# Two bf16 products on constants in each tile of the second FFN's expert loop

## The chip, the core and the metric

The program runs on one core of one Trainium2 chip. The metric is the device time of one execution in microseconds (us); lower is better. The core's engines run side by side and wait for each other on semaphores: TensorE (PE; its weight loads are listed as PEld), VectorE (DVE), ScalarE (ACT), GpSimd (POOL), and SyncE (SP), whose queue issues most of the transfers.

## What is computed

A graph network with four pairs of a graph layer and a mixture-of-experts FFN on 3125 nodes of 256 features. The change is in the second FFN. Each node goes to one of 32 experts with a hidden width of 64, a quarter of the feature width:

```python
def _L1_ffn_ref(x, router_w, router_b, W1, b1, W2, b2):
    logits = xf @ router_w.T + router_b
    idx = jnp.argmax(logits, axis=-1)
    w1t = jnp.take(W1, idx, axis=0)          # W1: (32, 256, 64)
    h = jax.nn.relu(jnp.einsum('nd,ndh->nh', xf, w1t) + jnp.take(b1, idx, axis=0))
    w2t = jnp.take(W2, idx, axis=0)          # W2: (32, 64, 256)
    out = jax.nn.relu(jnp.einsum('nh,nhd->nd', h, w2t) + jnp.take(b2, idx, axis=0))
```

## The kernel before

The stages run one after the other: a graph layer (`layer`), then `route`, `run_experts` and `combine` of an FFN, and so on. `route` picks an expert for each node and POOL scatters the normed rows to slots sorted by expert, in tiles of 128 slots that belong to one expert each. `run_experts` then works through the tiles. `combine` gathers the results back to the nodes.

`run_experts` serves the first FFN (`m0`: 8 experts, hidden 256), the second (`m1`: 32 experts, hidden 64, 56 tiles) and the fourth (`m3`: 16 experts, hidden 512). FP is the smaller of 128 and the hidden width, so it is 64 in `m1` alone. The tiles are a software pipeline over the engines. PE's step for tile c is written out by hand (lines 1428 to 1447):

- `turn(c + 1)`, line 1413: two transposes of the next tile's rows, as products with the identity, into `tp`. VectorE copies them to `xt` (line 1492).
- the up products of tile c, line 1437: weights `wa`, moving `xt`, into `hp`. In `m1` they fill 128 rows and 64 columns of the array. ScalarE makes `h` of `hp` (line 1471).
- `down(c - 1)`, line 1423: weights `h` of the tile before, moving `wb`, into `yp`. In `m1` they fill 64 rows and 128 columns. VectorE adds the bias and takes the maximum with zero into `yo` (lines 1500 and 1505), and ACT's queue stores `yo` to `results`.

So what PE needs in a step from VectorE (the copy of tile c) and from ScalarE (`h` of tile c - 1) was asked for a step earlier. An f32 product appears in the trace as two instructions: line 1437 gives 4 in a step of `m1`, line 1413 gives 2, line 1423 gives 2. SP loads each tile's `wa` and `wb` eight tiles ahead (lines 1389 and 1392, each waits for the down of an earlier tile) and the rows of four tiles in one transfer (line 1382). VectorE waits before its second tile for the table of second biases, `b2b` (line 1399 loads it). `over` runs the steps, the first eight unrolled and the rest in a loop of eight.

Of the kernel before, what the change touches and what calls it, by code (L numbers as in the profile page):

```python
# [16 lines left out]
BF16 = mybir.dt.bfloat16  # L17
# [7 lines left out]
P = 128  # L25
# [1304 lines left out]
def run_experts(nc, k, m, func, w1, b1, w2, b2, relu_out, slots, results, meanwhile):  # L1330


    sem, F, FP, FB, E, n = k.sem, m.F, m.FP, m.FB, m.E, m.tiles
# [18 lines left out]
    with ExitStack() as scope:  # L1352
# [3 lines left out]
        def bank(n, shape):  # L1356
            return scope.enter_context(nc.psum_tensor(f"{m.name}_x_{n}", shape, F32))
# [8 lines left out]
        b1_given, b1t = sb("b1_given", [rows_b1, FP]), sb("b1t", [FP, rows_b1])  # L1366
        turn_psum, h_psum, y_psum = bank("tp", [P, 2, 512]), bank("hp", [FP, 2, 512]), bank("yp", [P, 2, 512])
        b1_psum = bank("b1p", [FP, rows_b1])
        with nc.Block() as block:
            meanwhile(block)  # L1370

            @block.sync
            def _(sp):
                sp.dma_start(b1_given[:], b1.rearrange("e (b f) -> (e b) f", f=FP)).then_inc(s["b1_in"], 16)
                experts = []

                def step(c, u, i, first):
                    if u % DEEP == 0:
                        count = min(DEEP, n - c) if isinstance(c, int) else DEEP
                        if not first:  # L1380
                            sp.wait_ge(s["turned"], c - DEEP)
                        sp.dma_start(xin[:, u:u + count, :],
                                     slots[bass.ds(c * P, count * P), :].rearrange("(t p) f -> p t f", p=P))\
                            .then_inc(rows_in[u // DEEP], 16)
                        experts[:] = experts_from(mybir.EngineType.SP, c)
                    e, v = experts[u % DEEP], u % W
                    if not first or u >= W:
                        sp.wait_ge(s["down"], c - W + 1)
                    sp.dma_start(wa[:, v, :, :], w1[bass.ds(e, 1), :, :].rearrange("e (b p) f -> p (e b) f", p=P))\
                        .then_inc(loaded[v], 16)  # L1390
                    if not all_w2:
                        sp.dma_start(wb[:, v, :, :],
                                     w2[bass.ds(e, 1), :, :].rearrange("e (b p) f -> p (e b) f", p=FP))\
                            .then_inc(loaded[v], 16)
                    if first and u == 0:
                        if all_w2:
                            sp.dma_start(wb[:, :, :, :].rearrange("p e b f -> p (e b) f"),
                                         w2.rearrange("e (b p) f -> p (e b) f", p=FP)).then_inc(w2_in, 16)
                        sp.dma_start(b2b[:], b2.partition_broadcast(P)).then_inc(b2_in, 16)
                over(sp, n, ROUND, step)  # L1400

            @block.tensor
            def _(pe):
                pe.wait_ge(s["b1_in"], 16)
                nc.tensor.transpose(b1_psum[:], b1_given[:], k.ident[0:rows_b1, 0:rows_b1]).then_inc(s["b1_turned"], 1)

                def turn(c, u, i, early):
                    if u % DEEP == 0:
                        pe.wait_ge(rows_in[u // DEEP], (i + 1) * 16)
                    if not early:  # L1410
                        pe.wait_ge(s["turned_sb"], c - 1)
                    for b in range(KD):
                        mm = nc.tensor.transpose(turn_psum[:, u % 2, b * P:(b + 1) * P],
                                                 xin[:, u, b * P:(b + 1) * P], k.ident[:])
                    mm.then_inc(s["turned"], 1)

                def down(c, u, early, e):
                    pe.wait_ge(s["hidden"], c + 1)
                    if not early:
                        pe.wait_ge(s["out"], c - 1)  # L1420
                    for f in range(FB):
                        w = wb[:, bass.ds(e, 1), f, :].rearrange("p e f -> p (e f)") if all_w2 else wb[:, u % W, f, :]
                        mm = nc.tensor.matmul(y_psum[:, u % 2, 0:D], h[:, u % 2, f, :], w,  # L1423
                                              start=(f == 0), stop=(f == FB - 1))
                    mm.then_inc(s["down"], 1)


                def step(c, u, i, first):
                    if not (isinstance(c, int) and c == n - 1):
                        turn(c + 1, (u + 1) % ROUND, i + (u + 1) // ROUND, first and u == 0)  # L1430
                    pe.wait_ge(s["turned_sb"], c + 1)
                    pe.wait_ge(loaded[u % W], (i * (ROUND // W) + u // W + 1) * per_tile)
                    if not first or u >= 2:
                        pe.wait_ge(s["hidden"], c - 1)
                    for f in range(FB):
                        for b in range(KD):
                            mm = nc.tensor.matmul(h_psum[:, u % 2, f * P:(f + 1) * P],  # L1437
                                                  wa[:, u % W, b, f * FP:(f + 1) * FP],
                                                  xt[:, u % 2, b * P:(b + 1) * P], start=(b == 0), stop=(b == KD - 1))
                    mm.then_inc(s["up"], 1)  # L1440
                    if all_w2 and u % DEEP == 0:
                        start = first and u == 0
                        experts[:] = [None] * start + list(experts_from(mybir.EngineType.PE, c if start else c - 1))
                    if all_w2 and first and u == 1:
                        pe.wait_ge(w2_in, 16)
                    if not first or u >= 1:
                        down(c - 1, (u - 1) % ROUND, first and u <= 2, experts[u % DEEP] if all_w2 else None)
                experts = []
                turn(0, 0, 0, True)
                over(pe, n, ROUND, step, last_apart=True)  # L1450
                down(n - 1, (n - 1) % ROUND, False, experts_from(mybir.EngineType.PE, n - 1)[0] if all_w2 else None)

# [29 lines left out]

            @block.vector
            def _(dve):
                dve.wait_ge(s["b1_turned"], 1)
                nc.vector.tensor_copy(b1t[:], b1_psum[:]).then_inc(s["b1"], 1)

                def copy(c, u, early):
                    dve.wait_ge(s["turned"], c + 1)
                    if not early:  # L1490
                        dve.wait_ge(s["up"], c - 1)
                    nc.vector.tensor_copy(xt[:, u % 2, :], turn_psum[:, u % 2, 0:D]).then_inc(s["turned_sb"], 1)

                def finish(c, u, i, e):
                    dve.wait_ge(s["down"], c + 1)
                    if not isinstance(c, int) or c >= DEEP:

                        dve.wait_ge(stored[u % DEEP // 2], (2 * i + u // DEEP) * 16)
                    to = yo[:, u % DEEP, :]
                    ins = nc.vector.tensor_tensor(to, y_psum[:, u % 2, 0:D],  # L1500
                                                  b2b[:, bass.ds(e, 1), :].rearrange("p e f -> p (e f)"), ALU.add)
                    if relu_out:
                        ins.then_inc(s["sum"], 1)
                        dve.wait_ge(s["sum"], c + 1)
                        ins = nc.vector.tensor_scalar(to, to, 0.0, None, ALU.max)
                    ins.then_inc(s["out"], 1)

                def step(c, u, i, first):
                    if not (isinstance(c, int) and c == n - 1):
                        copy(c + 1, u + 1, first and u == 0)  # L1510
                    if u % DEEP == 0:

                        start = first and u == 0
                        experts[:] = [None] * start + list(experts_from(mybir.EngineType.DVE, c if start else c - 1))
                    if not first or u >= 1:
                        finish(c - 1, (u - 1) % ROUND, i if u else i - 1, experts[u % DEEP])
                experts = []
                copy(0, 0, True)
                dve.wait_ge(b2_in, 16)
                over(dve, n, ROUND, step, last_apart=True)  # L1520
                finish(n - 1, (n - 1) % ROUND, (n - 1) // ROUND, experts_from(mybir.EngineType.DVE, n - 1)[0])
# [491 lines left out]
```

## Time and profile before

| | us |
|---|---|
| median of 3 runs | 4030.24 |
| range of the runs | 4023.66 to 4031.4 |
| the profiled execution | 3997.73 |
| its span, first to last instruction | 3995.8 |
| mean granted TensorE clock of it | 0.809 |

The profile is of one execution. Its own time is 1.9 us above its span, and 0.8% below the median of the runs. The granted clock is a share of the full 2.4 GHz: 1.00 is full, 0.50 is 1.2 GHz. Matmuls are pipelined, and each row's duration reaches to the modelled end of its last product, so that groups overlap in the rows; the distance from the start of one group to the start of the next is what counts.

### The profile page before, as it was taken

How to read it: one execution, taken by the hardware profiler on the slowest of the kernel's cores; microseconds unless marked ns; L12 is line 12 of the kernel's file. 1: busy time of each engine (PE TensorE's matmuls, PEld its weight loads, DVE VectorE, ACT ScalarE, POOL GpSimd, SP SyncE). 2: the span in 40 equal slices, each digit the busy share in tenths (PEclk: the TensorE clock that was granted, in tenths of full speed). 3: DMA queues.
4: the chain of work that ended last, by engine and by line, in shares of the span. 5: the costliest groups of instructions: out<-in, count | busy, mean ns of one | idle time of the engine just before them, and what ended most of it. 6: DMA issues, size and time to landing. Idle time of an engine off the chain costs nothing. (4 is left out here: it accounts for less than half of the span.)

```text
span 3995.8 us, 42625 instructions
## 1 busy us (share of the span) xinstructions
PE 2921.7 (73%) x12729; PEld 1717.6 (43%) x12730; DVE 1247.8 (31%) x4178; ACT 766.0 (19%) x1927; POOL 1561.7 (39%) x1107
## 2 busy tenths in 40 slices
PE   2344219889997482999899839599879499927980
PEld 1122104334446282444444515244469255526870
DVE  8899600004445334000300323300121500131126
ACT  4899500000002020100100101100133300012221
POOL 0788888836400574820650061583000300040005
PEclk6555559999996696999999755699889799958995
DMA  6899749679871394986897155599300344218983
GB/s 278 289 293 291 211 81 319 189 231 306 263 240 52 115 254 121 340 261 208 279 264 263 34 136 140 184 325 272 98 24 0 108 129 129 56 56 281 328 283 94
DMA packets 449643, 781.39 MB, mean 196 GB/s; under 512 B 157952, under 2 KB 298498, under 8 KB 439509
## 3 DMA queue, kind: packets, MB, share of 16 engines
q1 hardware_dynamic: 300372, 722.78, 52.1%
q0 software_dynamic: 124896, 33.44, 9.0%
q10 hardware_dynamic: 24224, 23.34, 1.7%
q8 instruction: 75, 1.23, 0.1%
q14 instruction: 76, 0.61, 0.0%
HBM read 604.33 MB, written 175.05 MB: 195 GB/s over the span
## 5 line engine op out<-in xcount | busy, mean ns | idle before, releaser
L789 PE MATMUL sum_psum<-abuf,y 128*128 128x512 f32 (+1 forms) x3500 | 1415.3, 564 | 320.1 <-ACT y L718 176.9
L789 PEld LDWEIGHTS sum_psum<-abuf,y 128*128 128x128 f32 x3500 | 627.1, 191 | 1088.8 <-issue 941.8
L561 POOL DMA_INDIRECT table_t<-sums,index_from x392 | 614.6, 1568 | 402.2 <-POOLq L1936 190.8
L561 POOL DMA_INDIRECT table_pairs<-sums,index_to x392 | 610.4, 1557 | 226.5 <-issue 116.3
L725 ACT ACTIVATE gathered<-sum_psum 128x512 f32<-128x512 f32 (+1 forms) x84 | 41.0, 540 | 1862.9 <-PE sum_psum L789 1862.9
L1137 POOL COPY y<-m_ybuf 128x256 f32 (+1 forms) x39 | 15.7, 402 | 759.8 <-ACT m_ybuf L1202 759.8
L1534 POOL DMA_INDIRECT m_c_rows<-results,slot_i x125 | 119.1, 953 | 474.6 <-PEq L1528 437.4
L789 PE MATMUL sum_psum<-abuf,acc 128*128 128x512 f32 (+1 forms) x700 | 290.0, 577 | 9.4 <-DMA abuf<-table_pairs 9.4
L1437 PE MATMUL m_x_hp<-m_x_xt,m_x_wa 128*128 128x128 f32 (+1 forms) x1720 | 255.4, 300 | 25.8 <-DMA m_x_wb<-in_L_ffn_W_dram 9.6
L1423 PE MATMUL m_x_yp<-m_x_wb,m_x_h 128*128 128x256 f32 (+2 forms) x860 | 252.9, 427 | 6.6 <-issue 6.6
L441 PE MATMUL merge_psum<-part,acc 128*128 128x6 bf16 x980 | 70.9, 167 | 241.8 <-DVE pass_on L515 124.0
L1471 ACT ACTIVATE m_x_h<-m_x_hp,m_x_b1t 128x128 f32<-128x128 f32 (+1 forms) x430 | 130.4, 367 | 582.8 <-PE m_x_hp L1437 574.7
L1437 PEld LDWEIGHTS m_x_hp<-m_x_xt,m_x_wa 128*128 128x128 f32 (+1 forms) x1720 | 221.8, 199 | 46.8 <-issue 26.6
L789 PEld LDWEIGHTS sum_psum<-abuf,acc 128*128 128x128 f32 x700 | 130.1, 201 | 165.2 <-issue 155.4
L441 PEld LDWEIGHTS merge_psum<-part,acc 128*128 128x128 bf16 x980 | 56.8, 104 | 325.0 <-issue 322.7
L485 DVE SCALAR_TENSOR_TENSOR acc<-row_psum,edge_key,acc 128x128 bf16<-128x128 f32 (+3 forms) x392 | 192.3, 546 | 1.4 <-PE row_psum L421 1.1
L465 ACT ACTIVATE away<-row_psum,edge_key 128x512 f32<-128x512 f32 x291 | 179.9, 699 | 63.6 <-PE row_psum L427 62.4
L469 ACT ACTIVATE acc<-away 128x512 bf16<-128x512 f32 x291 | 181.3, 648 | 0.0
L1423 PEld LDWEIGHTS m_x_yp<-m_x_wb,m_x_h 128*128 128x128 f32 (+1 forms) x860 | 162.5, 208 | 41.3 <-issue 27.5
L1323 POOL DMA_INDIRECT slots<-y,slot_i x125 | 125.0, 1000 | 100.6 <-DVE slot_i L1178 63.4
L835 DVE TENSOR_TENSOR acc<-out_psum,rows 128x256 f32<-128x256 f32 (+1 forms) x25 | 10.6, 423 | 427.7 <-PE out_psum L748 427.7
L1500 DVE TENSOR_TENSOR m_x_yo<-m_x_yp,acc 128x256 f32<-128x256 f32 x122 | 51.8, 425 | 279.3 <-PE m_x_yp L1423 256.6
(333 smaller groups left out, 2965.8 us busy)
## 6 DMA issues: line engine op xcount, KB each, us to landing
abuf<-table_pairs SPq DMA_DIRECT2D x750, 512.0 KB, 4.9
table_pairs<-zero SPq DMA_DIRECT2D x50, 1600.0 KB
table_t<-zero SPq DMA_DIRECT2D x25, 1600.0 KB
abuf<-table_t SPq DMA_DIRECT2D x150, 256.0 KB, 2.6
m_x_wa<-in_L_ffn_w_dram SPq DMA_DIRECT2D x65, 512.0 KB, 4.3
m_x_wb<-in_L_ffn_w_dram SPq DMA_DIRECT2D x65, 512.0 KB, 5.6
m_x_xin<-slots SPq DMA_DIRECT2D x44, 512.0 KB, 3.9
results<-m_x_yo ACTq DMA_DIRECT2D x88, 256.0 KB, 4.5
```

What stands on the lines that cost most here:

```text
L441: mm = nc.tensor.matmul(to, k.same[:, u % 2, at(j) + i * P:at(j) + (i + 1) * P], k.part[:, g, c.start + j, :], start=(j == i), stop=(u == ...
L465: nc.scalar.activation(k.away[:, j, :], next_rows(u + 1), ACT.Abs, bias=column(k.edge_key, u, j), scale=-1.0).then_inc(apart, 1)
L469: nc.scalar.activation(k.later[:, u % 3, j, :], k.away[:, j, :], ACT.Relu, bias=1.0, scale=-1.0, accum_out=column(k.more, u, j)).then_inc( ...
L485: nc.vector.scalar_tensor_tensor(k.same[:, u % 2, at(j):at(j + 1)], own_rows(u)[:, 0:(j + 1) * P], column(k.edge_key, u, j), k.mask[:, (BL ...
L561: nc.gpsimd.indirect_dma_start(table[:, :], bass.IndirectOffsetOnAxis(ap=index[:, g, j:j + 1], axis=0), k.sums[:, g, j, 0:width], None, co ...
L789: mm = nc.tensor.matmul(k.sum_psum[:, b % 2, f, 0:n], h[:, c, f * P:(f + 1) * P], operand(i % RING, c - q * QUART, n), start=(c == 0), sto ...
L1323: nc.gpsimd.indirect_dma_start(slots, bass.IndirectOffsetOnAxis(ap=k.slot_i[:, j:j + 1], axis=0), k.y[:, j // K, :], None).then_inc(s["lai ...
L1423: mm = nc.tensor.matmul(y_psum[:, u % 2, 0:D], h[:, u % 2, f, :], w, start=(f == 0), stop=(f == FB - 1))
L1437: mm = nc.tensor.matmul(h_psum[:, u % 2, f * P:(f + 1) * P], wa[:, u % W, b, f * FP:(f + 1) * FP], xt[:, u % 2, b * P:(b + 1) * P], start= ...
L1471: ins = nc.scalar.activation(h[:, u % 2, f, :], h_psum[:, u % 2, f * P:(f + 1) * P], func, bias=b1t[:, bass.ds(e * FB + f, 1)])
L1500: ins = nc.vector.tensor_tensor(to, y_psum[:, u % 2, 0:D], b2b[:, bass.ds(e, 1), :].rearrange("p e f -> p (e f)"), ALU.add)
L1534: nc.gpsimd.indirect_dma_start(rows[:, j % GROUP, :], None, results[0:m.tiles * P, :], bass.IndirectOffsetOnAxis(ap=k.slot_i[:, j:j + 1], ...
```

## The change

With FP below 128, which is `m1` alone, VectorE fills a tile `busy` of 128 x 512 bf16 with 0.5 at the start of the stage and counts a semaphore up, for which PE waits before its first instruction. In each step PE multiplies a 128 x 128 part of `busy` with all 512 columns of it, once after `turn(c + 1)` and once after the up products. Both write to a PSUM bank of their own that nothing reads. Nothing that is kept is computed otherwise than before.

```diff
+        narrow = FP < P
+        if narrow:
+            busy, busy_psum, busy_ready = sb("busy", [P, 512], BF16), bank("busyp", [P, 512]), sem(f"{m.name}_x_busy")
...
             @block.tensor
             def _(pe):
+                if narrow:
+                    pe.wait_ge(busy_ready, 1)
                 pe.wait_ge(s["b1_in"], 16)
...
                     if not (isinstance(c, int) and c == n - 1):
                         turn(c + 1, (u + 1) % ROUND, i + (u + 1) // ROUND, first and u == 0)
+                    if narrow:
+                        nc.tensor.matmul(busy_psum[:], busy[:, 0:P], busy[:], start=True, stop=True)
                     pe.wait_ge(s["turned_sb"], c + 1)
...
+                    if narrow:
+                        nc.tensor.matmul(busy_psum[:], busy[:, 0:P], busy[:], start=True, stop=True)
                     if not first or u >= 1:
                         down(c - 1, (u - 1) % ROUND, first and u <= 2, experts[u % DEEP] if all_w2 else None)
...
             @block.vector
             def _(dve):
+                if narrow:
+                    nc.vector.memset(busy[:], 0.5).then_inc(busy_ready, 1)
                 dve.wait_ge(s["b1_turned"], 1)
```

On PE, at the start of `m1`'s stage, the order of before is this (`tp` are the transposes, `hp` the up products, `yp` the down products; a row is one product with its output's shape):

```order
L1405 MATMUL m_x_b1p<-ident,m_x_b_given 64x32
L1413 MATMUL m_x_tp<-ident,m_x_xin 128x128 x4
L1437 MATMUL m_x_hp<-m_x_xt,m_x_wa 64x128 x2
L1413 MATMUL m_x_tp<-ident,m_x_xin 128x128 x2
L1437 MATMUL m_x_hp<-m_x_xt,m_x_wa 64x128 x2
L1423 MATMUL m_x_yp<-m_x_wb,m_x_h 128x256
```

And in the changed kernel, on PE at the same place:

```order
L1410 MATMUL m_x_b1p<-ident,m_x_b_given 64x32
L1418 MATMUL m_x_tp<-ident,m_x_xin 128x128 x4
L1437 MATMUL m_x_busyp<-m_x_busy 128x512
L1444 MATMUL m_x_hp<-m_x_xt,m_x_wa 64x128 x2
L1454 MATMUL m_x_busyp<-m_x_busy 128x512
L1418 MATMUL m_x_tp<-ident,m_x_xin 128x128 x2
L1437 MATMUL m_x_busyp<-m_x_busy 128x512
L1444 MATMUL m_x_hp<-m_x_xt,m_x_wa 64x128 x2
L1454 MATMUL m_x_busyp<-m_x_busy 128x512
L1428 MATMUL m_x_yp<-m_x_wb,m_x_h 128x256
```

One product on `busy` now stands between the transposes and the up products, and one between the up and the down products. The other engines keep their order; VectorE has one instruction more, ahead of its first copy.

## Rows read from the trace of the kernel before

**Rows 1.** The page: busy tenths and granted clock in 40 slices of 100 us
```profile
span 3995.8 us, 42625 instructions
...
PE   2344219889997482999899839599879499927980
...
PEclk6555559999996696999999755699889799958995
```

**Rows 2.** Busy time by stretch: start, middle of m0's loop, m1's start, its loop
```profile
core 0: us, PE busy (x) PEld busy (x) DVE busy (x) ACT busy (x) POOL busy (x), PEclk, DMA share, GB/s
...
1404.60:1408.40 3.80, 3.80 (x14) 3.33 (x15) 0.43 (x2) 0.63 (x2) 3.19 (x3) 0.50 1.10 349
1408.50:1531.00 122.50, 113.26 (x771) 101.56 (x770) 42.43 (x111) 34.45 (x110) 70.55 (x46) 1.00 0.87 222
2248.20:2569.00 320.80, 194.16 (x613) 117.53 (x614) 130.46 (x447) 38.48 (x91) 111.37 (x100) 0.50 0.40 110
2353.00:2366.00 13.00, 2.85 (x10) 1.72 (x10) 0.85 (x2) 0.36 (x1) 9.93 (x7) 0.50 1.05 352
2366.40:2519.00 152.60, 152.57 (x435) 81.86 (x436) 58.23 (x162) 19.64 (x55) 37.27 (x24) 0.50 0.54 135
```

**Rows 3.** One step of m1's loop, all engines in order of time
```profile
2402.36 0.69 PE L1413 MATMUL m_x_tp<-ident,m_x_xin 128*128 128x128 f32 x2
2402.68 0.42 DVE L1500 TENSOR_TENSOR m_x_yo<-m_x_yp,m_x_b2b 128x256 f32<-128x256 f32 x1 [1.36 <-PE m_x_yp L1423]
...
2402.98 1.12 PE L1437 MATMUL m_x_hp<-m_x_xt,m_x_wa 128*64 128x128 f32 x4
2403.14 0.29 DVE L1505 TENSOR_SCALAR m_x_yo<-m_x_yo 128x256 f32<-128x256 f32 x1
...
2403.35 0.42 DVE L1492 COPY m_x_xt<-m_x_tp 128x256 f32<-128x256 f32 x1
...
2404.02 1.22 PE L1423 MATMUL m_x_yp<-m_x_wb,m_x_h 64*128 64x256 f32 x2
2404.22 0.36 ACT L1471 ACTIVATE m_x_h<-m_x_hp,m_x_b1t 64x128 f32<-64x128 f32 x1 [2.44 <-PE m_x_hp L1437]
...
2405.17 0.69 PE L1413 MATMUL m_x_tp<-ident,m_x_xin 128*128 128x128 f32 x2
```

**Rows 4.** PE's waits from 2366 to 2520 us, all of them
```profile
PE m_x_hp L1437 <- DMA m_x_wb<-in_L_ffn_W_dram: 9.6, 1, 9.6
```

**Rows 5.** PE in order of time, start of m0's loop: its clock rises
```profile
1404.49 2.05 PE L1437 MATMUL m_x_hp<-m_x_xt,m_x_wa 128*128 128x128 f32 x8 [6.72 <-DMA m_x_wa<-in_L_ffn_w_dram]
1406.33 1.91 PE L1423 MATMUL m_x_yp<-m_x_wb,m_x_h 128*128 x4
1408.04 0.59 PE L1413 MATMUL m_x_tp<-ident,m_x_xin 128*128 128x128 f32 x2
1408.46 1.06 PE L1437 MATMUL m_x_hp<-m_x_xt,m_x_wa 128*128 128x128 f32 x8
...
1410.22 0.38 PE L1413 MATMUL m_x_tp<-ident,m_x_xin 128*128 128x128 f32 x2
1410.44 1.06 PE L1437 MATMUL m_x_hp<-m_x_xt,m_x_wa 128*128 128x128 f32 x8
1411.34 1.03 PE L1423 MATMUL m_x_yp<-m_x_wb,m_x_h 128*128 x4
1412.20 0.38 PE L1413 MATMUL m_x_tp<-ident,m_x_xin 128*128 128x128 f32 x2
```

**Rows 6.** Groups by line, 100 to 500 us: products on 16-bit operands
```profile
L441 PE MATMUL merge_psum<-part,acc 128*128 128x6 bf16 x870 | 63.2, 167 | 217.6 <-DVE pass_on L515 116.0 <-DVE acc L485 66.1 <-ACT acc L469 35.4
...
L421 PE MATMUL row_psum<-edge_h,pick 113*128 113x512 f16 x84 | 49.3, 587 | 0.0
```

**Rows 7.** The start of m1's stage, in order of time
```profile
2350.99 0.26 PE L1405 MATMUL m_x_b1p<-ident,m_x_b_given 32*64 32x32 f32 x1 [47.57 <-DMA m_x_b_given<-in_L_ffn_b_dram]
...
2355.06 1.11 PE L1437 MATMUL m_x_hp<-m_x_xt,m_x_wa 128*64 128x128 f32 x4
...
2366.43 1.09 PE L1437 MATMUL m_x_hp<-m_x_xt,m_x_wa 128*64 128x128 f32 x4 [9.64 <-DMA m_x_wb<-in_L_ffn_W_dram]
```

**Rows 8.** The end of m1's loop and the first gather of combine
```profile
2517.71 1.11 PE L1437 MATMUL m_x_hp<-m_x_xt,m_x_wa 128*64 128x128 f32 x4
...
2525.53 1.01 POOL L1534 DMA_INDIRECT m_c_rows<-results,slot_i  x1 [114.84 <-PEq L1528]
```

**Rows 9.** SP's issues in m1's loop, in order of time, from 2403.23 us
```profile
2403.23 0.38 SPq L1382 DMA_DIRECT2D m_x_xin<-slots  x1
2405.34 0.37 SPq L1389 DMA_DIRECT2D m_x_wa<-in_L_ffn_W_dram  x1
2405.80 0.48 SPq L1392 DMA_DIRECT2D m_x_wb<-in_L_ffn_W_dram  x1
```

## The prediction

> **What bounds the kernel now.** I read the page's slices first, to see where TensorE's clock is low while TensorE is busy: besides the start there is such a place at about 2350 to 2550 us [rows 1]. Busy time by stretch says what it is. From 2248.2 to 2569.0 us the granted clock is 0.50 throughout, and in the middle of that lies the expert loop of the second FFN (m1): 152.6 us in which PE is listed busy for 152.57 us, VectorE for 58.23, ScalarE for 19.64, and the transfers take a share of 0.54 [rows 2]. So this loop is PE's.
>
> Next I looked for the waits of PE that the change means to fill. One step in order of time shows none. VectorE's copy for the step's up products was made in the step before; in this step it runs at 2403.35, long before its reader at 2405.8. ScalarE's h comes at 2404.22 and is read by the down products of the next step at about 2406.8 [rows 3]. In the whole loop PE waits for another engine once, for a transfer, 9.6 us at its start [rows 4]. What sets the pace is PE's own issue. From one transpose to the next is 2.81 us: 0.62 for the two transposes, 1.04 for the four up instructions, 1.15 for the two down instructions.
>
> The first FFN (m0) runs the same loop at both clocks and tells how much of this is columns. At 0.50 its eight up instructions take 1.84 us and its four down instructions 1.71, or 0.427 for 256 columns, and so 0.213 for 128. At 1.00, ups take 0.90 for 8 (0.112 each), transposes 0.22 for 2 (0.11 each) and downs 0.86 for 4 (0.215 each) [rows 5]. For m1 that is, at 0.50, 2 x 0.213 + 4 x 0.213 + 2 x 0.427 = 2.13 us. The other 0.68 us of the 2.81 stand at the three places where the shape in the array changes (128 x 128, then 128 x 64, then 64 x 128): about 0.19 + 0.19 + 0.30. In m0 all shapes are 128 x 128 and the same boundaries cost nothing.
>
> **What the change adds.** (1) A fill of busy on VectorE and a wait of PE for it before PE's first instruction. PE's first instruction waits 47.57 us anyway, until a transfer lands at 2350.99, and VectorE has nothing else to do then [rows 7]. Price 0; uncovered it would be one short instruction, once.
>
> (2) Two products of 512 bf16 columns in each of 56 steps. The nearest row is one product of 512 f16 columns at clock 0.50, 587 ns from start to modelled end [rows 6]. The tail of a product overlaps the next: m0's four downs at 0.50 last 1.91 us, of which 4 x 0.427 are columns, so the tail is 0.20 [rows 5], which leaves about 0.39. I take 0.427 at 0.50 and 0.215 at 1.00, as for 256 f32 columns, which pass twice. Two of them are 0.85 or 0.43 us a step. No idle time of PE hides them, since there is none.
>
> (3) Boundaries of shape. The first product follows the transposes and has their shape, so the boundary to the up products only moves behind it. The second puts up (64 columns), busy (128 x 128), down (64 rows) in place of up, down: one boundary more. At 0.50 it costs 0.19, like the others; at least 0 if 16-bit operands need no such pause, at most 0.30.
>
> So with the clock unchanged the step becomes 2.81 + 0.85 + 0.19 = 3.85 us (bounds 3.66 and 4.0).
>
> (4) What it may give back: the clock. The trace shows full clock after a stretch without a pause. In m0 the clock was 0.50 while PE ran without pause from 1404.49 on, and at about 1408.4 it rose, to stay at 1.00 for the rest of that loop, small pauses included [rows 2, 5]. In m1 PE never runs a step without three pauses, and half of its columns meet a half-filled array. Two full-shape products make the step denser and fuller. That they lift the clock is what I don't know: no row shows it between these two cases.
>
> The Trainium skill ("TensorE: Matmul & The Clock Gate", "What's actually happening") says that the low clock is the default and that activity of the array lifts it; its table "Why this matters for your kernels" asks only that no idle gap be long. By that alone m1's loop of before, in which PE is hardly idle, would be at full clock already, and the products would be pure cost, 55 x 0.43 = 24 us. The rows disagree: 0.50 for all of the loop [rows 2]. So filling or short pauses count as well, and I weigh the chance by the rows alone.
>
> With the clock at 1.00 the step is, without pauses, 2 x 0.11 + 4 x 0.112 + 2 x 0.215 = 1.10, and 0.43 for the products: 1.53. Pauses at 1.00 are nowhere in the rows with a change of shape. They lie between 0 and what they are at 0.50, 0.68 + 0.19 = 0.87. I take 0.6, nearer to the upper end, since the same boundaries in the same loop cost 0.87 at 0.50, and part of a pause is the drain of the array. The step is 2.13 us (bounds 1.53 and 2.40).
>
> Is something else late at 2.13? VectorE needs 0.42 + 0.29 + 0.42 = 1.13 us a step, ScalarE 0.36 [rows 3]; SP issues two weight loads, 0.37 and 0.48 with a small pause, and a quarter of a row load, some 1.1 us [rows 9]. The transfers' share of 0.54 would become 0.54 x 2.81 / 2.13 = 0.71, below the 0.87 at which m0 ran [rows 2]. At 1.53 us it would be 0.99, so the low bound is also where the transfers would take over. Nothing bounds at 2.13.
>
> **The sum, against the profiled execution of 3997.73 us.** The first tile's products fall before PE's wait of 9.64 us for a transfer and cost nothing. 55 steps follow, from 2366.43 to 2517.71 us [rows 7, 8], and behind them combine starts at 2525.53, after the last results are stored, so a shorter loop moves all that follows. Clock lifted: 4 steps until it is, 4 x 1.04 = +4 us; 51 x (2.13 - 2.81) = -35; sum -31 us (bounds: at 1.53, 51 x -1.28 + 3 = -62; at 2.40, -21 + 5 = -16). That is 3967 us for the profiled execution. It lies 0.8% below the median of the runs, which I take as the base: 4030.24 - 31 = 3999 us.
>
> **The rivals.**
>
> The clock stays at 0.50, and the products are cost. For it: PE has no idle time to put them in; the pauses at changes of shape stay and one is added; three of now five groups are as before. Against it: the share of full-shape columns grows much. Price 55 x 1.04 = +57 us (bounds 55 x 0.85 = +47 and 55 x 1.2 = +66): 4087 us, in all runs. It decides where the clock does not rise within the loop. This is the case on the other side.
>
> The clock rises late, or falls back now and then. With 22 steps at 3.85 and 33 at 2.13 gain and loss cancel, 22 x 1.04 = 33 x 0.68 to a microsecond: 4030 us. For it: the pauses stay, and one is added. Against it: in m0 the clock, once up, stayed up for 122.5 us [rows 2], and the steps of m1 are all alike, so that what lifts it in one should lift it soon in another. The Trainium skill (the same page, "A second HAM failure mode: psum-queue depth-cycling") tells of a clock that goes up and down where TensorE has frequent short idles between groups; no row of m1 shows an up and down so far.
>
> The clock rises, but a boundary of shape costs as much or more than at 0.50, or the weight loads are late: 2.4 to 2.6 us a step, -16 to -6 us, 4014 to 4024 us. It counts as faster, since about 0.2% (8 us) is what a measurement of this kernel can tell from no change, apart from its upper end.
>
> **How the numbers follow.** Clock lifted early, 0.53 (of which pauses as at 0.50, 0.1); late or on and off, 0.07, half of it within 0.2%; clock at 0.50, 0.40. The likeliest is 3999 us; its own range is 3968 to 4020. Together: faster 0.54, within 0.2% 0.06, slower 0.40. Since the slow case holds 0.40, the range must take it in: from 3972, the lower bound but for its last microseconds, to 4092, which leaves out the upper part of the slow case.
>
> **What will show it.** In the loop's stretch the granted clock is 1.00 or 0.50; that alone decides the sign. The distance from one transpose to the next should be 2.1 us at 1.00 or 3.85 at 0.50; a value below 1.7 says that shape boundaries cost nothing at full clock. The first gather of combine comes some 31 us earlier, or 57 later. Nothing ahead of 2350 us moves. I am wrong if the busy products take other than 0.43 or 0.215 us each, if PE waits for VectorE or ScalarE in the loop of the changed kernel, or if a part outside the loop moves.

## The result and the profile after

| | before | with the change |
|---|---|---|
| median, us | 4030.82 (4 runs, 4023.66 to 4037.99) | 4079.25 (4 runs, 4072.71 to 4085.64) |
| profiled execution, us | 3997.73 | 4072.71 |
| ratio | | 1.012, 95% interval 1.0096 to 1.0144 |

The change makes the kernel 48 us slower. The forecast was 3999 us, and the case that came true is the first rival, "the clock stays at 0.50", which had 4087 us and a chance of 0.40.

Busy time of the changed kernel by stretch (columns as in [rows 2]): the loop from its second up products to its last, and its even middle.

```profile
2388.40:2592.00 203.60, 203.56 (x538) 93.64 (x538) 56.86 (x161) 19.60 (x54) 37.53 (x24) 0.50 0.40 101
2399.00:2585.00 186.00, 186.00 (x494) 85.42 (x492) 52.67 (x150) 17.78 (x49) 28.46 (x19) 0.50 0.37 98
```

The last three numbers of a line are the granted clock, the transfers' share and GB/s: the clock is 0.50 all along, as in the last of [rows 2]. The loop is 203.6 us long, and was 151.3 [rows 7, 8]. One step of it, in order of time, answers to [rows 3]:

```profile
2402.49 0.69 PE L1418 MATMUL m_x_tp<-ident,m_x_xin 128*128 128x128 f32 x2
...
2402.97 0.63 PE L1437 MATMUL m_x_busyp<-m_x_busy 128*128 128x512 bf16 x1
...
2403.54 1.12 PE L1444 MATMUL m_x_hp<-m_x_xt,m_x_wa 128*64 128x128 f32 x4
...
2404.59 0.61 PE L1454 MATMUL m_x_busyp<-m_x_busy 128*128 128x512 bf16 x1
...
2405.12 1.22 PE L1428 MATMUL m_x_yp<-m_x_wb,m_x_h 64*128 64x256 f32 x2
...
2406.27 0.69 PE L1418 MATMUL m_x_tp<-ident,m_x_xin 128*128 128x128 f32 x2
```

From transpose to transpose it is 3.78 us, where 2.81 stood before: 0.97 more in each of 54 steps is the 52.3 us to within rounding. No row of PE carries a wait: PE waits in this loop for an engine or a transfer only at its start, and at the stage's start the wait for the fill of `busy` is covered, as these rows of the changed kernel show (in brackets the idle time before an instruction and what ended it):

```profile
2371.74 0.48 DVE L1495 MEMSET m_x_busy<- 128x512 bf16 x1 [33.41 <-PEq L1183]
...
2373.20 0.23 PE L1410 MATMUL m_x_b1p<-ident,m_x_b_given 32*64 32x32 f32 x1 [47.62 <-DMA m_x_b_given<-in_L_ffn_b_dram]
...
2388.45 1.09 PE L1444 MATMUL m_x_hp<-m_x_xt,m_x_wa 128*64 128x128 f32 x4 [8.67 <-DMA m_x_wb<-in_L_ffn_W_dram]
...
2600.40 1.01 POOL L1545 DMA_INDIRECT m_c_rows<-results,slot_i  x1 [167.46 <-PEq L1539]
```

Between the second and the third of these rows the clock was up for a while, in front of the loop. Busy time by stretch from the first tile's work on (2375.8 us), through the wait of 8.67 us:

```profile
2375.80:2380.10 4.30, 3.97 (x13) 2.13 (x13) 0.42 (x1) 0.36 (x1) 3.44 (x3) 0.50 1.05 385
2380.20:2383.40 3.20, 0.00 (x0) 0.00 (x0) 0.00 (x0) 0.00 (x0) 2.67 (x2) 1.00 1.18 492
2383.60:2388.40 4.80, 0.00 (x0) 0.00 (x0) 0.42 (x1) 0.00 (x0) 2.99 (x2) 0.50 1.06 276
```

The work on the first tile, which has products on `busy` and no down products yet, is followed by a rise to 1.00. It comes when PE is already idle, and before the transfer lands the clock is back at 0.50. In the kernel before nothing of the kind is there: its clock is 0.50 in the same wait [rows 2]. So the change does lift the clock once, where it is worth nothing, and not in the loop.

The first gather of combine stands at 2600.40, 74.9 us later than in [rows 8]. Of these, 22 us are there before the stage begins (2373.20 against 2350.99 in [rows 7]). They come from a load of `gru_b` in the graph layer, ahead of the second FFN, which the waits of the two kernels show (total, times, longest). The first row is of before, the second of after:

```profile
PE m_turn_psum L1064 <- DMA gru_b<-in_L_gnn_bhh_dram: 21.6, 1, 21.6
```
```profile
PE m_turn_psum L1064 <- DMA gru_b<-in_L_gnn_bhh_dram: 43.9, 1, 43.9
```

This is not the change's. The changed kernel on another chip (e10 below) waits 20.4 us there, and one and the same kernel waits 20.6 us on one chip and 43.4 on another (e9 and e17). So the two profiled executions differ by 75 us, of which the change has about 53, and the medians by 48.

### The profile page after: what moved, and what is told of

Its sections match the earlier page's. It is cut to its first block and busy times, and to the rows that moved or that the text cites. A ratio compares the mean times of both kernels' runs of the same rounds, so it can differ in the third digit from the quotient of the medians.

```text
span 4070.6 us, 42851 instructions
## 1 busy us (share of the span) xinstructions
PE 2965.4 (73%) x12841; PEld 1723.0 (42%) x12842; DVE 1245.9 (31%) x4179; ACT 765.9 (19%) x1927; POOL 1561.5 (38%) x1107
```

## The experiments

All kernels below but e16 are made from the changed kernel and keep its fill. Up to e12 only the number, the place and the shape of the products on `busy` differ; what else e13 to e18 change is said with them. Only e18 leaves out something of the computation. "2+2" means two products after the transposes and two after the up products; the change is 1+1. A step is the distance from one tile's transposes to the next's in the profiled execution. The loop runs from the second up products to the last. "Against before" goes by the medians of the same comparison, whose before lies at 3994 to 3998 us for e1 to e12, on three chips, and at 4029 to 4033 for e13 to e18, on a fourth. The medians scatter by some 6 us around the difference of the loops (e1 +17.2 against +23.1, e6 -33.4 against -26.7), so small differences between kernels are read from steps and loops. Where the clock reads 1.00, the loop's first two to four steps are still at 0.50.

| kernel | products in a step | clock in the loop | step, us | loop, us | against before, us | ratio (95%) |
|---|---|---|---|---|---|---|
| before | 0+0 | 0.50 | 2.81 | 151.3 | | |
| the change | 1+1 | 0.50 | 3.78 | 203.6 | +48.4 | 1.0096 to 1.0144 |
| e10, the same again | 1+1 | 0.50 | 3.78 | 203.6 | +57.5 | 1.0120 to 1.0153 |
| e1 | 1+0 | 0.50 | 3.24 | 174.4 | +17.2 | 1.0026 to 1.0064 |
| e2 | 2+0 | 0.50 | 3.67 | 197.5 | +47.6 | |
| e3 | 36, once | 1.00, then 0.50 | 2.81 | 150.6 | -0.9 | 0.9984 to 1.0018 |
| e4 | 2+2 | 1.00 | 2.54 | 140.4 | -11.1 | 0.9955 to 0.9990 |
| e12 | 2+1 | 1.00 | 2.33 | 130.1 | -18.2 | 0.9944 to 0.9974 |
| e7 | 2+2 on 64 rows | 0.50 | 4.44 | 239.0 | +87 | one run |
| e8 | 2+2, 64 columns | 1.00 | 2.41 | 133.3 | -14 | one run |
| e5 | 2+2 in 8 steps, then 0+0 | 1.00, then 0.50 | 2.81 | 151.3 | -1.5 | 0.9989 to 1.0007 |
| e9 | ... then 1+0 | 1.00, then 0.50 | 3.24 | 166.8 | +17.9 | 1.0035 to 1.0060 |
| e6 | ... then 1+1 | 1.00 | 2.11 | 124.6 | -33.4 | 0.9900 to 0.9941 |
| e11 | as e6, the second product of each step with 64 columns | 1.00 | 2.01 | 118.8 | -28.6 | 0.9917 to 0.9943 |
| e13 | e5, longer `yo` | 1.00, then 0.50 | 2.81 | 145.7 | -5.6 | 0.9971 to 1.0002 |
| e14 | e9, longer `yo` | 1.00 | 1.79 | 113.7 | -38.1 | 0.9869 to 0.9908 |
| e15 | e11, longer `yo` | 1.00 | 2.01 | 114.5 | -33.3 | 0.9891 to 0.9926 |
| e16 | before, longer `yo` | 0.50 | 2.81 | 151.3 | -1.3 | 0.9982 to 1.0002 |
| e17, e9 again | as e9 | 1.00, then 0.50 | 3.24 | 169.1 | +16.7 | 1.0025 to 1.0055 |
| e18 | e13, one read less | 1.00, then 0.50 | 1.58, then 2.81 | 128.3 | -29.3 | 0.9898 to 0.9949 |

### What a product costs, and where it stands

e1 keeps the first of the two products, e2 puts both behind the transposes, e10 is the changed kernel once more. The edit of e1:

```diff
-                        nc.tensor.matmul(busy_psum[:], busy[:, 0:P], busy[:], start=True, stop=True)
+                        for _ in range(1):
+                            nc.tensor.matmul(busy_psum[:], busy[:, 0:P], busy[:], start=True, stop=True)
...
-                    if narrow:
-                        nc.tensor.matmul(busy_psum[:], busy[:, 0:P], busy[:], start=True, stop=True)
                     if not first or u >= 1:
```

> Of the two products of the change only the one behind the transposes is left. Theory (the products are pure cost at the low clock, and PE waits for nobody): granted clock 0.50 in the loop, a step of 2.81 + 0.43 = 3.24 us, so 55 x 0.43 = 24 us above the kernel before. Rival (the cost sits where the shape in the array changes, and this product adds no such place): the step stays near 2.81 and the time within 5 us of before.

> Both products stand behind the transposes, so no change of shape is added. Theory: clock 0.50, a step of 2.81 + 2 x 0.43 = 3.67 us, 47 us above before, some 6 us below the changed kernel. Rival (the added pause between up and down is what kept the clock low): granted clock 1.00 within the loop, a step of about 2.1 us, some 30 us below before.

> The changed kernel itself, beside the others on one chip, 12 executions. Theory (two products a step never lift the clock in the loop; only the dense start does, once, ahead of PE's wait): every execution some 50 us above before, none below it. Rival (it depends on where in the chip's counting the steps fall, as the scatter of the run with both products behind the transposes suggests): most executions 50 us above, a few 30 us below before.

One product is 3.24 - 2.81 = 0.43 us, the second beside it 3.67 - 3.24 = 0.43. Set apart, as the change has it, it takes 3.78 - 3.24 = 0.54: the boundary of shape that it adds costs 0.11. So the cost is there in every step, and the gain is not. e1's loop is 23.1 us longer than before's, as expected, and its median only 17.2 above. e2's four executions are not alike: 4044.1, 4045.0, 4048.6 and 3967.9. The profiled one has clock 0.50. The short one's mean granted clock was 0.895 against 0.874 and 0.875 in the others. No execution of before is above 0.881, and the kernels that run the loop at 1.00 have up to 0.901, so that the clock most likely rose in the short one, but no trace of it is there. None of the eight executions of the changed kernel (four each time) came below before.

### Does any number of products lift the clock?

e3 issues 36 products while PE waits for the second tile's weights, and none in the steps; e4 has two at either place, e12 two and one. The edit of e4, which stands at both places:

```diff
-                        nc.tensor.matmul(busy_psum[:], busy[:, 0:P], busy[:], start=True, stop=True)
+                        for _ in range(2):
+                            nc.tensor.matmul(busy_psum[:], busy[:, 0:P], busy[:], start=True, stop=True)
```

> No product in the loop; instead 36 of them in a row, once, in the 10 us in which PE waits for the second tile's rows (VectorE waits for the biases). Theory (the clock rises on unbroken full-shape work and, once up, holds at less than it needs to rise, as it does in m0's loop): granted clock 1.00 through m1's loop, a step of 1.5 to 1.9 us, 50 to 70 us below before. Rival (the loop of m1 can't hold the clock, whatever came ahead): clock back at 0.50 after a few steps, a step of 2.81 us, 0 to 3 us above before for the end of the burst.

> Twice the products of the change: two behind the transposes, two behind the up products. If the change failed because it adds too little full-shape work, this is more of it: granted clock 1.00, a step of 1.10 + 4 x 0.215 + about 0.6 = 2.6 us, 10 us below before. If the pauses keep the clock down whatever stands between them: clock 0.50, a step of 3.78 + 0.85 = 4.63 us, 100 us above before.

> Three products in every step, two behind the transposes, one behind the up products. Theory (the change lacks just a little full-shape work): clock 1.00 from one of the first steps, a step of 2.11 + 0.22 = 2.33 us, 20 us below before, in every execution. Rival (four were needed): clock 0.50, a step of 4.2 us, 77 us above before.

PE in e4, in order of time, at the start of the loop:

```profile
2369.99 1.06 PE L1438 MATMUL m_x_busyp<-m_x_busy 128*128 128x512 bf16 x2
2370.98 1.12 PE L1445 MATMUL m_x_hp<-m_x_xt,m_x_wa 128*64 128x128 f32 x4
2372.03 1.03 PE L1456 MATMUL m_x_busyp<-m_x_busy 128*128 128x512 bf16 x2
2372.99 0.97 PE L1428 MATMUL m_x_yp<-m_x_wb,m_x_h 64*128 64x256 f32 x2
2373.90 0.44 PE L1418 MATMUL m_x_tp<-ident,m_x_xin 128*128 128x128 f32 x2
2374.17 0.59 PE L1438 MATMUL m_x_busyp<-m_x_busy 128*128 128x512 bf16 x2
2374.70 0.65 PE L1445 MATMUL m_x_hp<-m_x_xt,m_x_wa 128*64 128x128 f32 x4
```

Two products take 1.0 us and then 0.59, four ups 1.12 and then 0.65: the clock rises at 2373.6 and stays for the loop. With three (e12) the same comes at 2376.2. So the loop can be lifted, two products a step are too few for it, and even four a step, at 2.54 us, cost less than none at 2.81.

PE in e3, the burst and what followed:

```profile
2355.70 8.44 PE L1438 MATMUL m_x_busyp<-m_x_busy 128*128 128x512 bf16 x35 [0.22 <-issue]
2366.61 0.62 PE L1445 MATMUL m_x_hp<-m_x_xt,m_x_wa 128*64 128x128 f32 x4 [2.47 <-DMA m_x_wb<-in_L_ffn_W_dram]
2367.16 1.04 PE L1428 MATMUL m_x_yp<-m_x_wb,m_x_h 64*128 64x256 f32 x2
2368.13 0.69 PE L1418 MATMUL m_x_tp<-ident,m_x_xin 128*128 128x128 f32 x2
2368.74 1.12 PE L1445 MATMUL m_x_hp<-m_x_xt,m_x_wa 128*64 128x128 f32 x4
```

The burst lifts the clock (the ups at 2366.61 take 0.62), PE is idle for 2.47 us behind it, and at 2367.4 the clock is back at 0.50. This run does not tell whether the idle time or the thin steps dropped it; e5 and the later ones do.

### Rows of the array or columns?

e7 gives the four products 64 rows, e8 64 columns; each still moves 512 columns of data. Cut down to the product itself, the edits are:

```diff
-nc.tensor.matmul(busy_psum[:], busy[:, 0:P], busy[:], start=True, stop=True)
+nc.tensor.matmul(busy_psum[:], busy[0:64, 0:P], busy[0:64, :], start=True, stop=True)      # e7
+nc.tensor.matmul(busy_psum[0:64, :], busy[:, 0:64], busy[:], start=True, stop=True)        # e8
```

> Four products in every step as in the run that lifted the clock, but each on 64 of the 128 rows (64 x 128 weights, 64 rows moving); as many columns stream. If the rows that are filled count for the clock: it stays at 0.50, a step of 4.6 us or more, 100 us above before. If only the time in which columns stream counts: clock 1.00, a step of about 2.6 us, some 10 us below before.

> Four products in every step, each with 128 x 64 weights (128 rows, 64 columns of the array). If what is filled of the array counts as rows times columns: clock 0.50, a step of 4.6 us, 100 us above before. If the array's columns don't count: clock 1.00, a step of about 2.6 us, some 10 us below before.

Busy time by stretch, e7's and then e8's:

```profile
2384.00:2584.00 200.00, 200.00 (x542) 86.76 (x541) 47.82 (x135) 16.43 (x46) 21.07 (x14) 0.50 0.33 88
```
```profile
2384.00:2490.00 106.00, 106.00 (x529) 57.81 (x528) 46.64 (x132) 15.96 (x44) 22.76 (x15) 1.00 0.63 163
```

In both PE is busy for every microsecond of the stretch. With 64 rows the clock stays at 0.50, with 64 columns it is 1.00. The pauses do not explain it: e7 has as many changes of shape in a step as e4, four, and e4 is lifted. At the start of the stage e7 differs too: the clock is 0.50 throughout PE's wait there, where it is 1.00 for a while in e1, e2, e4, e8 and the changed kernel. That sets `m1`'s own products apart: its ups leave columns empty, its downs leave rows empty, and the start of the stage, where a single product on `busy` for each of the first two tiles was enough in e1, has no downs. Both kernels ran once, 4085 and 3984 us, far apart. What the ups and the downs by themselves count for was not measured.

### Once it is up, what holds it?

e5, e6 and e9 have 2+2 in the first eight steps, which are unrolled, and then none, 1+1 or 1+0. The loop of steps differs in nothing else. e11 is e6 with 64 columns in the second product.

```diff
-                        nc.tensor.matmul(busy_psum[:], busy[:, 0:P], busy[:], start=True, stop=True)
+                        for _ in range(2 if first else 1):      # e6; 0 in e5; 1 and 0 in e9
+                            nc.tensor.matmul(busy_psum[:], busy[:, 0:P], busy[:], start=True, stop=True)
```

> Four products a step (two in each place) in the first eight steps only, none in the other 48. Theory (the change fails at lifting the clock, not at holding it; once up, the loop holds it by its own work): granted clock 1.00 from about the third step to the end, a step of 2.54 - 4 x 0.215 = 1.68 us without products, loop 48 x 1.13 = 54 us shorter, 50 us below before. Rival (without products the loop drops the clock, as it did behind the one burst): 0.50 again from the ninth step or a few later, steps of 2.81 us, within 5 us of before.

> Four products a step in the first eight steps, then the two of the change in the other 48. Theory (two products are too few to lift the clock but enough to hold it): clock 1.00 from about the third step, a step of 2.54 - 2 x 0.215 = 2.1 us, some 32 us below before. Rival (two products can't hold it either): clock back at 0.50, steps of 3.78 us, 45 us above before, like the changed kernel.

> Four products a step in the first eight steps, then one (behind the transposes) in the other 48. Theory (the fall without products came of PE's stall for VectorE, which waited for a store; one product a step covers for it): clock 1.00 to the end of the loop, a step of 1.57 + 0.22 = 1.8 us plus stalls, 40 us below before. Rival (one is too few to hold it): clock 0.50 from within the loop, steps of 3.24 us, 15 to 22 us above before.

> As the primed kernel with the two products of the change, but the second of them has 128 x 64 weights, the shape of the up products ahead of it, so that one boundary of shape fewer is there. Theory (a boundary of shape costs 0.06 to 0.1 us at full clock): a step of 2.03 to 2.05 us instead of 2.11, 35 us below before, 3 us below the primed kernel. Rival (it is the wait for stores that ends last by then): the same time as the primed kernel, within 1 us.

e6 runs the steps of the change at full clock: first busy time by stretch, then one step of PE.

```profile
2384.00:2484.00 100.00, 97.66 (x462) 49.06 (x460) 48.60 (x138) 16.69 (x47) 17.09 (x11) 1.00 0.62 168
```
```profile
2406.28 0.65 PE L1445 MATMUL m_x_hp<-m_x_xt,m_x_wa 128*64 128x128 f32 x4
2406.87 0.39 PE L1456 MATMUL m_x_busyp<-m_x_busy 128*128 128x512 bf16 x1
2407.19 0.70 PE L1428 MATMUL m_x_yp<-m_x_wb,m_x_h 64*128 64x256 f32 x2
2407.81 0.44 PE L1418 MATMUL m_x_tp<-ident,m_x_xin 128*128 128x128 f32 x2
2408.09 0.38 PE L1438 MATMUL m_x_busyp<-m_x_busy 128*128 128x512 bf16 x1
2408.40 0.65 PE L1445 MATMUL m_x_hp<-m_x_xt,m_x_wa 128*64 128x128 f32 x4
```

The step is 2.11 us, the whole 33 us below before. The same steps that cannot lift the clock keep it. Without products (e5) and with one (e9) it falls back, and in both behind an idle time of PE. This is PE and VectorE in e9, around the fall at 2396.9:

```profile
2392.59 0.38 PE L1438 MATMUL m_x_busyp<-m_x_busy 128*128 128x512 bf16 x1
2394.36 0.65 PE L1445 MATMUL m_x_hp<-m_x_xt,m_x_wa 128*64 128x128 f32 x4 [1.39 <-DVE m_x_xt L1505]
...
2397.41 1.11 PE L1445 MATMUL m_x_hp<-m_x_xt,m_x_wa 128*64 128x128 f32 x4 [1.19 <-DVE m_x_xt L1505]
```
```profile
2393.22 0.42 DVE L1513 TENSOR_TENSOR m_x_yo<-m_x_yp,m_x_b2b 128x256 f32<-128x256 f32 x1 [3.19 <-DMA results<-m_x_yo]
2393.68 0.29 DVE L1518 TENSOR_SCALAR m_x_yo<-m_x_yo 128x256 f32<-128x256 f32 x1
2393.89 0.42 DVE L1505 COPY m_x_xt<-m_x_tp 128x256 f32<-128x256 f32 x1
```

VectorE waits 3.19 us for a store to free one of the four tiles of `yo`; queued behind that is its copy of `xt`, and PE waits 1.39 us for the copy. One step later PE is idle for another 1.19 us, from 2396.22 on, and within that the clock falls. At 0.50, in the kernel before, VectorE never waits for a store. Either this stall drops the clock, or the steps hold too little. (In e6 and e11 the same wait is there, in all 7.3 and 9.8 us of VectorE's time, with PE idle for up to 1.0 and 1.3 us, and the clock holds.)

### The stall or the thin steps

e13 to e16 give `yo` eight tiles in `m1`: e13 from e5, e14 from e9, e15 from e11, and e16 from the kernel before. The semaphores of the stores grow along. Parts of the edit, some lines cut to what changes:

```diff
+    Y = 2 * DEEP if FP < P else DEEP
...
-sb("yo", [P, DEEP, D])
+sb("yo", [P, Y, D])
...
-                    if not isinstance(c, int) or c >= DEEP:
+                    if not isinstance(c, int) or c >= Y:
```

> Products in the first eight steps only (two at each place), none afterwards, as in e5, but with eight tiles of the result buffer yo instead of four, so that VectorE is not held by a store. Theory (the stall that a store puts on VectorE, and through it on TensorE, is what drops the clock): no stall, the clock stays at 1.00 to the end, a step takes about 1.57 us, and the kernel is about 55 us below before. Rival (the steps without products are themselves too thin to keep the clock): it falls back to 0.50 within some steps, a step takes 2.81 us again, and the kernel is within 8 us of before. A step of 1.57 us asks for more stores a microsecond, so a later stall than in e5 would leave the two unseparated; the place of the fall against the first stall tells.

> As e9 (products in the first eight steps, then one behind the transposes) with eight tiles of yo. Theory of the stall: the clock stays, a step takes 1.79 us, about 42 us below before. Rival (one product a step is too little): it falls to 0.50, a step 3.24 us, 15 to 20 us above before.

> As e11 (products in the first eight steps, then the change's two, the second with a weight of 64 columns) with eight tiles of yo. Both theories: the clock stays at 1.00; steps of 2.01 us with fewer of 2.4 to 3.1, so up to 8 us below e11, 28 to 40 us below before.

> The kernel before with eight tiles of yo and no products. At a step of 2.81 us no store holds VectorE long, so both theories expect before's time within 4 us; it is the control for the three others.

With one product a step, e14 now holds the clock from 2406 us to the loop's end, with steps of 1.79 us, and lies 38 us below before. Busy time by stretch:

```profile
2408.00:2508.00 100.00, 93.57 (x465) 49.59 (x465) 52.47 (x151) 18.14 (x50) 26.40 (x17) 1.00 0.69 181
```

VectorE no longer waits for a store in it. All of PE's waits from 2408 to 2509 us are these (total, times, longest):

```profile
PE m_x_hp L1446 <- DVE m_x_xt L1506: 5.9, 11, 0.9
PE m_x_hp L1446 <- issue: 0.5, 1, 0.5
```

PE's idle times that are left, at most 0.9 us, have another source: in every fourth step VectorE reads the expert numbers of four tiles into registers between its copy and its addition, and is late by it (e18, below, has no such steps). The buffer alone is worth nothing (e16). e13, with no product, still falls. It had two waits of PE for the copy, both from those reads:

```profile
2419.52 0.65 PE L1446 MATMUL m_x_hp<-m_x_xt,m_x_wa 128*64 128x128 f32 x4 [0.96 <-DVE m_x_xt L1506]
...
2427.27 0.65 PE L1446 MATMUL m_x_hp<-m_x_xt,m_x_wa 128*64 128x128 f32 x4 [1.30 <-DVE m_x_xt L1506]
```

The clock fell at 2429.2, behind the second. The first is instructive: e5 has an idle time of 0.99 us at the same place, the third step without products, and fell 1.8 us behind it, while e13 ran on at 1.00 for nearly ten more. That stall of e5's, which the longer `yo` did not remove, was thus most likely the reads' and not a store's, and its length alone does not decide whether the clock falls; no row shows what tells the two apart. Since e9 and e14 ran on different chips, e17 repeats e9 on e14's chip. e18 goes on from e13 and takes VectorE's reads out; it leaves out that each tile gets its own expert's second bias, and adds expert 0's to all.

```diff
-                    if u % DEEP == 0:
+                    if u % DEEP == 0 and not narrow:
                         start = first and u == 0
                         experts[:] = [None] * start + list(experts_from(mybir.EngineType.DVE, c if start else c - 1))
                     if not first or u >= 1:
-                        finish(c - 1, (u - 1) % ROUND, i if u else i - 1, experts[u % DEEP])
+                        finish(c - 1, (u - 1) % ROUND, i if u else i - 1, 0 if narrow else experts[u % DEEP])
```

> The kernel of e9 once more (products in the first eight steps, then one a step; four tiles of yo), since e9 and e14 ran on different chips. Theory (the stall from the store drops the clock): the same as e9, a fall to 0.50 right after a step over 3 us, steps of 3.24, 15 to 25 us above before. Rival (e9 and e14 differ by the chip and not by the buffer): the clock holds, steps of 1.79, 25 to 40 us below before.

> As e13 (eight tiles of yo, products in the first eight steps only, none after), and VectorE no longer reads the expert numbers of four tiles in one go, which in e13 still held it for 2.5 us in every fourth step. Left out for this: it adds expert 0's second bias to all tiles of m1. Theory (only stalls drop the clock): no step over 1.8 us, the clock stays at 1.00, the loop takes about 54 x 1.57 + 20 = 100 us instead of 151, the kernel is some 50 us below before. Rival (steps with no products are themselves too thin): it falls to 0.50 without a stall ahead of it, steps of 2.81, the loop 140 to 147 us, 4 to 10 us below before.

e17 falls as e9 did, at 2431.9, one step behind an idle time of 1.61 us, and is 17 us above before; the buffer and not the chip holds e14. VectorE waits 3.29 us there, for which the profile names no releaser; that it is the store, as in e9, follows from e14, where nothing but the buffer differs.

```profile
2430.41 0.65 PE L1445 MATMUL m_x_hp<-m_x_xt,m_x_wa 128*64 128x128 f32 x4 [1.61 <-issue]
```

e18's rows on PE tell the rest. First busy time by stretch from 2416 us, then, in order of time, what comes ahead of its fall at 2459.7:

```profile
2416.00:2455.00 39.00, 38.04 (x191) 21.37 (x190) 25.00 (x69) 8.35 (x24) 21.63 (x14) 1.00 0.88 209
2462.00:2520.00 58.00, 58.00 (x166) 30.76 (x165) 21.37 (x62) 7.61 (x21) 0.00 (x0) 0.50 0.46 137
```
```profile
2455.54 0.41 PEld L1446 LDWEIGHTS m_x_hp<-m_x_xt,m_x_wa 128*64 128x64 f32 x4 [0.17 <-issue]
...
2456.12 0.70 PE L1429 MATMUL m_x_yp<-m_x_wb,m_x_h 64*128 64x256 f32 x2
...
2458.71 0.44 PE L1419 MATMUL m_x_tp<-ident,m_x_xin 128*128 128x128 f32 x2 [1.89 <-DMA m_x_xin<-slots]
...
2459.07 0.65 PE L1446 MATMUL m_x_hp<-m_x_xt,m_x_wa 128*64 128x128 f32 x4
...
2459.65 1.21 PE L1429 MATMUL m_x_yp<-m_x_wb,m_x_h 64*128 64x256 f32 x2
```

For some 40 us, 23 steps, the kernel's own steps with no product at all run at 1.00, at 1.58 us each, with a wait of 0.6 us among them. Then PE waits 1.89 us for a load of rows (the transfers' share is 0.88 by now), and within a microsecond the clock is at 0.50, where the second row shows it for good, though PE is never idle again. Neither expectation was quite right: the steps are not too thin, but something stalled them after all.

The longest idle times of PE at the raised clock, by kernel, in us, and what the clock did:

| products in a step | held | fell within 3 us of its end |
|---|---|---|
| 0+0 | 0.61 (e18), 0.96 (e13, its first) | 0.99 (e5), 1.30 (e13, its second), 1.89 (e18) |
| 1+0 | 0.9 (e14) | 1.39 (e9), 1.61 (e17) |
| 1+1 | 1.0 (e6), 1.3 (e11), 0.2 (e15) | |

Whether the clock holds thus goes with the stalls, and with how much the steps have to spare for them; 0.96 and 0.99 us on two sides of the table say that the length of one stall is not all of it. What is shown for 1+0 by e14 against e17, and for 0+0 by e18's first 23 steps, is that a step which does not lift the clock in the loop can keep it. That the stall itself and nothing else dropped it in e5, e13 and e18 is seen in their order of time alone, since no kernel of this kind without any stall was run.

## Why the prediction was wrong, point by point

- **The fill and its wait, at nothing.** Right: 0.48 us on VectorE, done 1.0 us before the transfer lands that PE waits for.
- **The products, 0.427 us each at 0.50 and 0.215 at 1.00.** Right: 0.43 (e1, e2) and 2.54 - 2.33 = 0.21 (e4 against e12). No idle time of PE hides them, as was said.
- **The added boundary, 0.19 us, bounds 0 and 0.30.** Inside, but too dear: 0.11. So the step was 3.78 us and not 3.85. The sum also counts a step too many: 151.3 us at 2.81 are 54 steps and not 55. So the loop took 52.3 us more, where the rival's sum had 57. The medians give 48.4 and, in e10, 57.5.
- **That the products lift the clock, 0.53.** This is the step that failed, and with it the sign. I had one row where the clock rises, `m0`'s start, all 128 x 128, and one where it doesn't, `m1`'s, and put the changed kernel nearer to the first since its steps become "denser and fuller". How dense they had to be no row could say; the runs put the changed kernel just below. In the loop three products lift (e12) and two do not, or most likely once in four executions where both stand together (e2). The changed kernel did lift the clock once, in the work on the first tile, and lost it in the 8.67 us that PE then waits for weights. With two products in the steps the loop holds a clock that it is given (e6), so a change that only took this wait away might have done; that was not tried. What I left out of the weighing is that filled rows and filled columns might not count alike. e7 and e8 show that they don't, and the downs, with their 64 rows, are the longest group of `m1`'s step.
- **The step at full clock, 2.13 us, and "nothing bounds at 2.13".** The first is right though the changed kernel's loop never had that clock: 2.11 in e6, 2.01 with one boundary less (e11). The 0.6 us of pauses in it was a choice between 0 and 0.87, so that this is luck in part; 2.11 leaves 0.58. The same working for a step without products, with three boundaries in place of four, gives 1.10 + 0.6 x 0.68 / 0.87 = 1.57, and e18 has 1.58. The second half is wrong in small: at that pace VectorE comes late, by the store of `yo` and by its reads of expert numbers, which made some steps of e6 2.4 to 3.1 us, and the clock fell behind such a store in e9. I had compared VectorE's work of 1.13 us a step with 2.13, and not the time that a store holds one of four tiles.
- **The rival of a late or unsteady clock, 4030 us, 0.07.** Not seen in the changed kernel's loop, but real in its neighbours: e5, e9 and e13 go up and come down. The Trainium skill ("TensorE: Matmul & The Clock Gate", "A second HAM failure mode: psum-queue depth-cycling") tells of short idles between groups that make the clock go up and down. The traces agree in part: in e5, e9, e13, e17 and e18 a fall followed idle times of 0.99 to 1.89 us, but none of these loops went up again by itself. That page's table "Why this matters for your kernels", which asks that TensorE be kept busy and that no idle gap be long, does not describe this loop: here the clock was at 0.50 with PE never idle (before, the change, e7).
- **What would show it.** The transposes' distance said 3.85 for this case, measured 3.78; the combine's first gather was to come 57 us later, and came 53 later measured from the stage's start. "Nothing ahead of 2350 us moves" failed by 22 us, for a load whose time differs between chips for one and the same kernel.

## What to carry to other kernels

Cover work for TensorE's clock pays or costs by a step function, and where it stands on the steep side can't be read from the profile of before: try two or three amounts, and several executions of each, rather than one. Lifting the clock and holding it are two different needs. Where the clock only has to be lifted, put many products in a few steps at the start, few or none later, and first take away the stalls of the neighbours that a faster TensorE brings to light: e14 does so, and beats the kernel before by 1.1% where the change as given loses 1.2%. Fill all rows of the array with the extra products: four of 64 rows did nothing here, four of 64 columns lifted the clock.

## What was new about the hardware

- What lifts the clock and what holds it differ. One product a step does not lift it in the loop (e1, 0.50 from the second tile to the last) and holds it (e14, 1.00 for 100 us); the same goes for two (the change, e6), and for none over 23 steps (before, e18).
- The same products did lift it in the work on the first tile, in which no down products stand: 1.00 from 2380.2 to 2383.4 us with the change, while PE was already idle, and 0.50 again before the wait ended. It is not there in before and not in e7.
- Four products of 64 rows a step leave it at 0.50 with PE busy in 200.00 of 200 us (e7); four of 64 columns lift it (e8, 1.00).
- Idle times of PE of 1.0 to 1.9 us were all that stood ahead of the falls inside the loop, and 2.5 us ahead of e3's. One of 0.96 us (e13) passed without a fall, where one of 0.99 at the same place (e5) was followed by one.
- Going from one shape to another in the array costs at full clock as well: 2.11 - 2.01 = 0.10 us where e11 spares one such change (its second product also loads weights of half the columns, which no run sets apart), and 0.48 us are left in a step of 1.58 whose columns take 1.10.
